# Low part of the turned rows taken from PSUM by VectorE, in a local-attention layer on one Trainium2 core

## The reference, cut to what matters

```python
xn = _layernorm(x, axis=-1)
x = x + _L3_attn_ref(xn, Wq, Wk, Wv, Wo) + _L3_ffn_ref(xn, ln_gamma, ln_beta, fc1..., fc2...)

def _L3_attn_ref(x, Wq, Wk, Wv, Wo):
    q = (x @ Wq.T).reshape(B, T, H, D).transpose(0, 2, 1, 3)     # H = 16 heads of D = 16
    k = (x @ Wk.T)...; v = (x @ Wv.T)...
    out = _block_local_attn(q, k, v, 128)     # softmax over own and previous block of 128 keys
    return out.transpose(0, 2, 1, 3).reshape(B, T, C) @ Wo.T
```

## Time and profile before

| | us |
|---|---|
| median of 3 runs | 3110.12 |
| lowest, highest | 3103.7, 3117.47 |
| the profiled execution's own time | 3088.66 |
| its span in the trace | 3086.9 |

### The profile page before, as it was taken

One profiled execution on the slowest core, in us unless ns is written; L12 is line 12 of the kernel. 1 busy time (PEld: TensorE's weight loads), 2 busy tenths in 40 slices (PEclk: granted clock), 3 DMA queues, 4 the chain that ended last, 5 costly groups with the idle time before them and its releaser, 6 DMA issues.

```text
span 3086.9 us, 53060 instructions
## 1 busy us (share of the span) xinstructions
PE 2795.7 (91%) x15430; PEld 1758.9 (57%) x15431; DVE 1856.3 (60%) x4495; ACT 1385.5 (45%) x2009; POOL 340.2 (11%) x355
## 2 busy tenths in 40 slices
PE   5999999999988888888879999999999579999998
PEld 2455455545544444444437777776666456666666
DVE  5655655665546777777746777772112456665663
ACT  1633544453342555555544555532223144444443
POOL 0000000000000000000021111220111322222220
PEclk7999999999997999999989999999999789999999
DMA  7424532542602222222214111122221233333330
GB/s 218 131 93 120 158 109 77 164 137 81 164 2 91 71 70 69 63 63 70 62 58 161 44 43 54 48 89 71 101 68 58 89 96 103 105 104 104 99 99 19
DMA packets 155932, 279.84 MB, mean 91 GB/s; under 512 B 24704, under 2 KB 82432, under 8 KB 148832
## 3 DMA queue, kind: packets, MB, share of 16 engines
q1 hardware_dynamic: 143248, 244.91, 26.4%
q0 software_dynamic: 10464, 28.59, 3.0%
q10 hardware_dynamic: 2160, 5.61, 0.6%
HBM read 179.34 MB, written 99.68 MB: 90 GB/s over the span
## 4 chain that ended last, share of the span: by engine, by line
PE 69%; DVE 12%; issue 6%; DMA 6%; ACT 4%; POOL 2%; SPq 1%; DVEq 0%; ACTq 0%; POOLq 0%
PE bank_u L561 6%; PE pair L601 5%; PE pair L545 5%; PE bank L1923 4%; PE pair L702 4%; PE pair L2073 3%; DVE nmax L873 3%; PE pair L3013 3%; PE bank L2528 3%; PE bank_m L2977 3%; PE pair L746 3%; PE bank L2977 3%; PE bank L522 3%; PE pair L1421 2%; DMA k_a<-parts_dram 2%
## 5 line engine op out<-in xcount | busy, mean ns | idle before, releaser
L779 ACT ACTIVATE probs<-pair 128x1024 f32<-128x1024 f32 x512 | 501.2, 1021 | 200.4 <-PE pair L545 199.5
L873 DVE TENSOR_REDUCE nmax<-bank 128x1 f32<-128x512 f32 x664 | 441.7, 685 | 195.6 <-PE bank L522 147.3
L873 DVE TENSOR_REDUCE nmax<-bank_m 128x1 f32<-128x512 f32 x360 | 246.4, 685 | 113.2 <-PE bank_m L522 67.3
L561 PE MATMUL bank_u<-probs,vext 128*32 128x512 f32 x2048 | 284.8, 629 | 0.6 <-ACT uraw L766 0.5
L522 PE MATMUL bank<-k_a,q_a 96*128 96x512 f32 x336 | 173.2, 550 | 24.3 <-DMA k_a<-parts_dram 21.0
L545 PE MATMUL pair<-q_a,k_a 98*128 98x512 f32 x512 | 170.4, 439 | 17.5 <-ACT probs L779 12.2
L2221 DVE CUSTOM_DVE_ANT_0 bank<-bank,mask_q 128x128 f32<-128x128 f32 (+1 forms) x320 | 118.8, 421 | 88.9 <-PE bank_m L1963 71.7
L760 ACT ACTIVATE mrow<-bank 8x512 f32<-8x512 f32 x87 | 50.1, 576 | 238.4 <-PE bank L531 238.4
L545 PEld LDWEIGHTS pair<-q_a,k_a 98*128 98x128 f32 x512 | 88.0, 196 | 111.4 <-ACT probs L779 65.7
L1394 PE MATMUL bank<-k,q 62*128 62x512 f32 x302 | 113.5, 479 | 26.5 <-DVE nmax L873 26.5
L2073 PE MATMUL pair<-fc,hid 128*128 128x256 f32 x512 | 131.5, 395 | 6.3 <-ACT probs L2114 6.3
(11 more groups left out here) (455 smaller groups left out, 5813.3 us busy)
## 6 DMA issues: line engine op xcount, KB each, us to landing
parts_dram<-parts SPq DMA_DIRECT2D x64, 512.0 KB
q<-parts_dram SPq DMA_DIRECT2D x126, 128.0 KB
q_a<-parts_dram SPq DMA_DIRECT2D x31, 512.0 KB
k_a<-parts_dram SPq DMA_DIRECT2D x31, 512.0 KB
xs<-xres SPq DMA_DIRECT2D x24, 512.0 KB, 3.0
xl<-xs SPq DMA_DIRECT2D x24, 512.0 KB, 3.9
x_in<-xg SPq DMA_DIRECT2D x74, 128.0 KB, 2.0
yg_dram<-y_out POOLq DMA_DIRECT2D x72, 128.0 KB, 2.0
```

The source lines that it names most:

```text
L561: ins = nc.tensor.matmul(bank_u[32 * h:32 * h + 32, :], vext[:, kt, kv(g, h), :], probs[:, kt % 2, h * SEQ:(h + 1) * SEQ], start=(kt == 0) ...
L779: nc.scalar.activation(probs[:, kt % 2, hp * 2 * SEQ:hp * 2 * SEQ + n], st.tile(l, name)[:, 0:n], ACT.Exp).then_inc(st.free["act"].sem, 1)
L873: nc.vector.tensor_reduce(nmax[:, g % 2, qt, h:h + 1], sc.tile(l, name)[:], AX, ALU.max, negate=True).then_inc(sc.free["dve"].sem, 1)
```

## The change

Four things are done.

- ScalarE's second, full copy of `T` is dropped. The first copy signals a new semaphore, `turned_high3`.
- VectorE subtracts `xnT_high` from the PSUM tile `T` itself, when `turned_high3` has come, and it is now VectorE that frees the tile: in `st_plan3` the reader of `T` is "dve".
- TensorE waits before Q0 for `turned_high3` only, and for VectorE (the free of `T`) before Q0's third pass.
- The passes are taken in another order in all uses of `three_passes` of this layer: high x high, then the pass with the other operand's low part, and the pass with the low part of the second argument last (for Q and K that is `xnT_low`).

```diff
 def st_plan3(front, back):
-    return parts_of(front, back, ("back", [("T2", "act"), ("V", "dve")] + e3_uses(0) + e3_uses(1)), ("front", [("T", "act")]),
+    return parts_of(front, back, ("back", [("T2", "act"), ("V", "dve")] + e3_uses(0) + e3_uses(1)), ("front", [("T", "dve")]),
...
-        turned_low = sig("turned_low", [0, 0, 0, (1, 1)], "vector")
+        turned_low = sig("turned_low", [0, 0, 0, (0, 1)], "vector")
+        turned_high3 = sig("turned_high3", [0, 0, 0, (1, 0)], "scalar")
...
-                passes = ((0, 0), (0, 1), (1, 0))
+                passes = ((0, 0), (1, 0), (0, 1))
                 for n, (i, j) in enumerate(passes):
+                    if n == 2:
+                        before_low()
...
+            def turned_parts():
+                pe.wait_ge(*done(st, l, it, "T"))
...
                 if front and i == 0:
-                    pe.wait_ge(*turned_low.at(l, it, turned_low.per[l]))
+                    pe.wait_ge(*turned_high3.at(l, it, 1))
                 if front:
-                    dense(name, w_high[:, i % 2, :, :], w_low[:, i % 2, :, :], i // 2, xnT_high, xnT_low)
+                    dense(name, w_high[:, i % 2, :, :], w_low[:, i % 2, :, :], i // 2, xnT_high, xnT_low,
+                          turned_parts if i == 0 else lambda: None)
...
                 act.wait_ge(*st.filled(l, it, "T"))
-                nc.scalar.activation(xnT_high[:, :, :].rearrange("p k n -> p (k n)").bitcast(F32R), st.tile(l, "T")[:], ACT.Copy)
-                nc.scalar.activation(xnT[:, :, :].rearrange("p k n -> p (k n)"), st.tile(l, "T")[:],
-                                     ACT.Copy).then_inc(st.free["act"].sem, 1)
+                nc.scalar.activation(xnT_high[:, :, :].rearrange("p k n -> p (k n)").bitcast(F32R), st.tile(l, "T")[:],
+                                     ACT.Copy).then_inc(turned_high3.sem, 1)
...
-                dve.wait_ge(*done(st, l, it, "T"))
-                nc.vector.tensor_tensor(xnT_low[:].bitcast(F32R), xnT[:], xnT_high[:], ALU.subtract).then_inc(turned_low.sem, 1)
+                dve.wait_ge(*turned_high3.at(l, it, 1))
+                nc.vector.tensor_tensor(xnT_low[:, :, :].rearrange("p k n -> p (k n)").bitcast(F32R), st.tile(l, "T")[:],
+                                        xnT_high[:, :, :].rearrange("p k n -> p (k n)"), ALU.subtract).then_inc(st.free["dve"].sem, 1)
```

More of the change, by code:

```diff
@@ L1916, in pe3, with three_passes, dense @@
             front, back = FRONT[l], BACK[l]
-            def three_passes(dst, lefts, rights, first=True, last=True):
-                passes = ((0, 0), (0, 1), (1, 0))
+            def three_passes(dst, lefts, rights, before_low=lambda: None):
+                passes = ((0, 0), (1, 0), (0, 1))
                 for n, (i, j) in enumerate(passes):
+                    if n == 2:
+                        before_low()
                     for k in range(KT):
                         ins = nc.tensor.matmul(dst, lefts[i](k).bitcast(F32R), rights[j](k).bitcast(F32R),
-                                               start=(first and n == 0 and k == 0), stop=(last and n == 2 and k == KT - 1))
+                                               start=(n == 0 and k == 0), stop=(n == 2 and k == KT - 1))
                 return ins
-            def dense(name, high, low, m, right_high, right_low):
+            def turned_parts():
+                pe.wait_ge(*done(st, l, it, "T"))
+            def dense(name, high, low, m, right_high, right_low, before_low=lambda: None):
                 for s in sc.vacated(l, it, name):
@@ L1931, in dense @@
                 three_passes(sc.tile(l, name)[:], [lambda k: high[:, k, m * P:(m + 1) * P], lambda k: low[:, k, m * P:(m + 1) * P]],
-                             [lambda k: right_high[:, k, :], lambda k: right_low[:, k, :]]).then_inc(sc.full.sem, 1)
+                             [lambda k: right_high[:, k, :], lambda k: right_low[:, k, :]], before_low).then_inc(sc.full.sem, 1)
             def hidden(i):
```

## The result

The kernel after takes 3128.63 us (median of 6 executions, 3127.02 to 3134.18), the kernel before in the same session 3115.71 us (6, 3103.7 to 3123.18). The ratio is 1.0056, with a 95% interval of 1.0040 to 1.0072: slower, and just beyond the 0.5% that I had called the limit of what can be told from no change. I had forecast 3116.0 us, +5.9 us over before, for which 3110.1 was known then; the two medians here lie 12.9 us apart.

The account below looks back on a forecast made before the run. TensorE, busy 91% of the span, and the chain of waits through T and T2 were taken to set the time. -2.7 - 2.2 + 10.8 = +5.9 us on 3110.1 gave 3116.0 us, range 3100 to 3129.

Parts of the forecast that it names:

- Part one: T in a MAIN3 round, 7 rounds: without ScalarE's second copy Q0 starts 0.38 us earlier, 2.7 us gained in all.
- the rival in which the whole copy comes off: Gains arrive in full: 6.7 us in MAIN3, 3.2 in PRE3, net +0.9, 3111.0 us; chance 0.06.
- The PSUM source: VectorE's subtraction with one source in PSUM: costed at nothing, bounds -0.1 and +0.2 us on each of 8.
- Part two: T in PRE3, once: Q0 2.2 us earlier, all let through; bounds 0 (late DMA or GpSimd) and 3.2 us.
- Part three: Round start, 6 borders: T2 also waits for VectorE's addition to OUT, 1.80 us later each, 10.8 us lost.
- a rival with a chance of 0.12: At 6 borders the added wait also brings TensorE's clock down: 6 to 13 us more, 3122 to 3129 us; chance 0.12.
- Part four: Order of the passes, same matmuls and shapes: nothing, bounds of -1 and +1 us over the layer.

## Why the prediction was wrong

The direction and the place were right, the size was not: +5.9 us forecast, +23.3 in layer 3 of the profiled pair, and 0.40 to 0.72% (12 to 22 us) by the ratio. The pair is one execution of each, so the terms below are exact for it and less so for the kernels.

- **Part one, right.** -0.38 us a round forecast, 0.37 measured at Q0; T to oc, over the seven rounds, gave 2.0 of the 2.7 us, with one fall of the clock more than before in it. The forecast that E(2,0) would wait for VectorE and hold Q0 held too. Q0 ahead of it gained 0.3 us a round more; the rival in which the whole copy comes off had asked for 0.57 (0.95 - 0.38).
- **The PSUM source, right.** 1224 ns against 1226. By the errata table that the prediction weighed ("VectorE: DVE Perf Modes" of the Trainium skill) it would be 65 ns more; the trace doesn't agree for this operation either.
- **Part two, wrong in size.** Q0 came earlier by the 2.2 us (1.08 against 3.32 behind the first copy), and the last store was issued 12.3 us after T against 15.3, so 3 us of head start reached it. T to T2, however, is 41.71, 43.76 and 42.31 us in the three kernels without the new T (before, the order alone, the wait alone), and 41.96, 40.16, 41.07, 41.15 and 40.87 in five with it: 42.6 against 41.0 in the mean, some 1.5 us gained with a scatter of 1. The store took 4.29, 7.22, 5.04 us in the first three and 7.65, 5.73, 6.71, 6.66, 6.62 in the five. The pair of before and after happens to lie at two ends, so that it shows +0.25 us where -2.2 was forecast. The prediction let "the whole 2.2 us through" and kept the DMAs for a bound; part of it belonged off. What makes the store longer stays open.
- **Part three, the step that failed.** The mechanism was as foretold: a second wait at six borders, met in the round behind PRE3, with nothing to cover it. The price "1.80 a border, 10.8 in all" was mis-sized three times. The direct shift is 2.03 (oc to T2 from -0.52 to +1.51): I gave the released matmul the 0.05 us of handover seen at `values`, and it took 0.28 (2590.19 + 1.23 = 2591.42 to 2591.70). `hT_low` grew by 0.45 and I had it shift unchanged. And the clock fell, which I had set aside as a rival with a chance of 0.12: of the 1.95 us a round between T2 and T, 0.5 is `hT_low` by the run with the second stretch filled, and the remaining 1.45 the clock. 12.2 + 3.0 + 8.7 = 23.9 us where 10.8 stood; with 0.25 + 0.42 - 1.2 of the other rows, 23.3. The clock's part is the least certain: with the wait alone the five middle rounds had 1.0 us a round from T2 to T over the 29.6 without it, of which 0.5 is again `hT_low`.
- **Why I set the clock aside.** I wrote that TensorE would "idle another 1 us" ahead of E(0,1). My own numbers said otherwise: `vext` shifts by 1.80 and `values` by 1.3, so the idle stretch between them grows from 0.95 to about 1.45 us, and with the longer `hT_low` to 1.9 (2.00 measured), which is as long as the stretch in POST3 that I had cited as one behind which the clock falls.
- **Part four, right.** The order of the passes is worth 0.

The rival's own reckoning was near: 6 to 13 us for the clock, 3122 to 3129 in all. That the total fits is partly luck, since the kernel before, measured beside the kernel after, took 5.6 us more than the 3110.1 it was added to. It also looked at the wrong stretch: filling the first shows that the falls don't hang on that one alone.

## What to carry to other kernels

Where a ring's wait is compiled from counts, changing who frees one use can add a wait at another use of the tile, in a loop stage where nothing has changed: look there first, and drop it where the tile's real predecessor is covered by another wait. Price a delayed start by all that lies downstream in relation to it: what stays in place (a GpSimd addition, queued matmuls) now meets it at another point, and an idle stretch is the difference of two shifts. Where the change makes an idle stretch as long as one behind which the trace shows a fallen clock, the fall is a likely term of the sum (here it came at 11 of 12 such borders in two kernels). And work that is moved on GpSimd can land on VectorE's: look at both engines where it arrives.

## What the runs showed of the hardware

- The granted clock fell to its lower level in rounds in which TensorE is busy over 90% of the time (72.62 of 79.26 us, 0.51 over 6.8 us of it), behind idle stretches of 1.87 and 2.00 us. It did so at all six borders of the kernel after and at five of the six with the wait alone. With the first stretch filled it still fell; with the second filled it didn't fall there, and then fell some 39 us later in most rounds (48.5 us behind T2's start instead of 9.4), behind a stretch of 0.78 us. By what the chip decides this is open.
- VectorE's subtraction of two SBUF tensors takes 1225 ns with no GpSimd instruction beside it. It took 1.42 us where a GpSimd addition that had started first still ran for 0.34 us, and 1.87 us where it ran for 0.80 us; a GpSimd addition that started second took 3.12 us instead of 2.39 for 0.90 us of overlap. Each time the later one is longer by the overlap less some 0.15 us, and the earlier one keeps its length. VectorE's steps of 0.17 us grew to 3.20 and 2.27 us in the same way. "GPSIMD Engine Reference" of the Trainium skill, section "Specifications", says that GpSimd's SBUF interfaces are shared with VectorE, with contention for instructions with two SBUF inputs. This case's traces agree.
- A matmul behind an unmet wait instruction followed 0.28 us after the release; a matmul that carried its wait itself, 0.05 us. All six borders show the same; what makes the difference was not tested alone.
- The unchanged layers 0 to 2 took from 2448.7 to 2470.8 us in different executions, nearly the size of the effect studied. One profiled pair must be compared by stretches.
